# The cosine half of the rotary turn does the exchange of 64-dimension parts, and row sends move behind it

## The reference

```
def _rotate_half(x):
    d = x.shape[-1] // 2
    return jnp.concatenate([-x[..., d:], x[..., :d]], axis=-1)
...
q = q * cos + _rotate_half(q) * sin
k = k * cos + _rotate_half(k) * sin
...
scores = jnp.einsum('bqhd,bkhd->bhqk', q, k) * scale
```

## Time and profile before

| | |
|---|---|
| median of 3 runs | 1418.35 us (1413.24 to 1418.37) |
| profiled execution | 1411.39 us |
| its span, first to last instruction | 1409.6 us |
| mean granted clock of PE | 0.960 |
| PE busy | 1264.9 us, 90% |
| DVE busy | 1051.0 us, 75% |
| ACT busy | 854.4 us, 61% |
| POOL busy | 694.4 us, 49% |

### The profile page before, as it was taken

How to read it: one execution, slowest core, us unless ns; L and a number is a source line. 1 busy time by engine, 2 the same in 40 slices (tenths; PEclk the granted TensorE clock), 3 DMA queues, 4 the chain that set the end, 5 groups by cost and what they waited for, 6 DMA issues and landing times. The chain is left out here.

```text
span 1409.6 us, 28399 instructions
## 1 busy us (share of the span) xinstructions
PE 1264.9 (90%) x8780; PEld 1125.1 (80%) x8780; DVE 1051.0 (75%) x2191; ACT 854.4 (61%) x1956; POOL 694.4 (49%) x718
## 2 busy tenths in 40 slices
PE   3899999999999999999989989972997999999965
PEld 2789789889889888978978878862665999999854
DVE  3778677777787768879877878846224999999956
ACT  2666566565566556566656656634114999999832
POOL 4433433433443443344464455413713888888830
PEclk8999999999999999999999999975998999999979
DMA  7676676675467775577576577612305888888868
GB/s 241 166 184 158 172 180 157 175 200 149 120 167 191 195 197 142 140 197 181 155 198 178 131 180 194 182 59 44 107 30 156 271 271 274 269 271 268 258 203 264
DMA packets 204439, 256.48 MB, mean 182 GB/s; under 512 B 11130, under 2 KB 177694, under 8 KB 204340
## 3 DMA queue, kind: packets, MB, share of 16 engines
q1 hardware_dynamic: 193300, 229.92, 60.3%
q0 software_dynamic: 11040, 25.30, 5.5%
HBM read 90.42 MB, written 169.72 MB: 185 GB/s over the span
## 5 line engine op out<-in xcount | busy, mean ns | idle before, releaser
L764 DVE TENSOR_REDUCE neg_max<-scores 128x1 f32<-128x256 f32 (+7 forms) x256 | 193.0, 754 | 150.4 <-PE scores L880 148.5
L536 ACT ACTIVATE pt_hi<-pt 128x512 fp32r<-128x512 f32 (+3 forms) x384 | 174.7, 490 | 190.7 <-PE pt L889 189.0
L509 ACT ACTIVATE probs<-scores,neg_max 128x256 f32<-128x256 f32 (+7 forms) x256 | 190.2, 743 | 55.8 <-DVE neg_max L764 55.4
L469 POOL TENSOR_TENSOR turned<-turned,turn_sin 128x512 f32<-128x512 f32 x80 | 102.9, 1286 | 230.3 <-DVE turn_sin L708 230.3
L789 PE MATMUL o_ps<-pt_hi,v_hi 128*128 128x256 f32 (+1 forms) x640 | 193.6, 303 | 21.5 <-DVE o_lo L728 21.2
L720 DVE TENSOR_TENSOR pt_lo<-pt,pt_hi 128x512 fp32r<-128x512 f32 (+3 forms) x384 | 200.7, 551 | 13.5 <-ACT pt_hi L536 10.3
L790 PE MATMUL o_ps<-pt_lo,v_hi 128*128 128x256 f32 (+1 forms) x640 | 179.6, 281 | 0.0
L791 PE MATMUL o_ps<-pt_hi,v_lo 128*128 128x256 f32 (+1 forms) x640 | 179.3, 280 | 0.0
L466 POOL TENSOR_TENSOR turned<-taken,cos 128x512 f32<-128x512 f32 x80 | 104.1, 1301 | 144.9 <-ACT taken L519 144.7
L889 PE MATMUL pt<-ident,probs 128*128 128x128 f32 x1152 | 169.5, 274 | 5.7 <-DVE pt_lo L720 4.4
L1422 POOL DMA_INDIRECT results_dram<-y_sb,dest x134 | 148.6, 1109 | 33.7 <-issue 27.3
(11 more groups left out here) (250 smaller groups left out, 3668.9 us busy)
## 6 DMA issues: line engine op xcount, KB each, us to landing
rows_dram<-empty SPq DMA_DIRECT2D x64, 2096.2 KB
up_raw<-in_up SPq DMA_DIRECT2D x69, 368.0 KB
x_in<-rows_dram SPq DMA_DIRECT2D x68, 258.0 KB
parts<-results_dram SPq DMA_DIRECT2D x16, 768.0 KB, 9.8
down_raw<-in_down SPq DMA_DIRECT2D x69, 128.0 KB
down_raw<-in_down_tail SPq DMA_DIRECT2D x69, 112.0 KB
w_raw<-in_w SPq DMA_DIRECT2D x8, 768.0 KB, 16.5
wo_raw<-in_wo SPq DMA_DIRECT2D x8, 512.0 KB, 19.4
```

The source lines that it names most:

```text
L509: nc.scalar.activation(probs[:, at_probs(k, m), 0:w], scores_ps[m % 2][:, score_cols(m)], ACT.Exp, bias=neg_max[:, m % 4:m % 4 + 1], accum ...
L536: nc.scalar.activation(pt_hi[m // 2 % 2][:, a:z, P * (m % 2):P * (m % 2) + P], pt_ps[c % 2][:, 0:P * (z - a)].rearrange("p (k q) -> p k q" ...
L764: nc.vector.tensor_reduce(neg_max[:, n % 4:n % 4 + 1], scores_ps[n % 2][:, score_cols(n)], AX.X, ALU.max, negate=True).then_inc(max_made, 1)
```

## The change

POOL's cosine is now two instructions over 64 partitions each. They read one half of the partitions and write the other, with a wait between them, and DVE's sine is one instruction over 128 partitions without an exchange. DVE does a key's sine at the same place of the step as a query's, ahead of the reciprocal and of the addition to `resid`. Ahead of each first cosine instruction POOL waits until everything that it issued before is complete: its additions, its lower parts, and the landing of every row send. The sends are placed anew. In the first half they stood at every second step (49, 51, ..., 95); now there are two in neighbouring steps out of each four (50, 51, 54, 55, ..., 95). The other 24 stand in round 3 from its step 42 on, in three of four steps up to step 55 and in each step after it.

```
-EARLY_FILL = {step: f for f, step in enumerate([2 * STEPS + 49 + 2 * f for f in range(SENDS // 2)]
-                                               + [3 * STEPS + 41 + 2 * f for f in range(GT)]
-                                               + [3 * STEPS + 48 + f for f in range(SENDS // 2 - GT)])}
+EARLY_FILL = {step: f for f, step in enumerate([2 * STEPS + 50 + 4 * (f // 2) + f % 2 for f in range(SENDS // 2)]
+                                               + [3 * STEPS + n for n in range(41, 69) if n > 55 or n % 4 != 1])}
...
                         pool.wait_ge(proj_taken, now(k, len(ROPES), r + 1))
-                        pool.wait_ge(turn_split, now(k, len(ROPES), r - 1))
-                        nc.gpsimd.tensor_tensor(turned[r % 2][:], taken[r % 2][:], cos[:, pos], ALU.mult).then_inc(cos_made, 1)
-                        pool.wait_ge(cos_made, now(k, len(ROPES), r + 1))
+                        pool.wait_ge(turn_made, made["turn"])
+                        pool.wait_ge(turn_split, made["split"])
+                        for b in range(RING_ROWS):
+                            if made[b] > 0:
+                                pool.wait_ge(rows_sent[b], 16 * made[b])
+                        if not first:
+                            pool.wait_ge(x_split, made["x"])
+                            pool.wait_ge(w_split, made["w"])
+                            pool.wait_ge(wo_split, made["wo"])
+                        nc.gpsimd.tensor_tensor(turned[r % 2][0:64], taken[r % 2][64:128], cos[64:128, pos], ALU.mult).then_inc(cos_made, 1)
+                        pool.wait_ge(cos_made, 2 * now(k, len(ROPES), r) + 1)
+                        nc.gpsimd.tensor_tensor(turned[r % 2][64:128], taken[r % 2][0:64], cos[0:64, pos], ALU.mult).then_inc(cos_made, 1)
+                        pool.wait_ge(cos_made, 2 * now(k, len(ROPES), r + 1))
+                        made["turn"] += 1
                         pool.wait_ge(sin_made, now(k, len(ROPES), r + 1))
...
-                nc.vector.tensor_tensor(turn_sin[r % 2][0:64], taken[r % 2][64:128], sin[64:128, pos], ALU.mult)
-                nc.vector.tensor_tensor(turn_sin[r % 2][64:128], taken[r % 2][0:64], sin[0:64, pos],
-                                        ALU.mult).then_inc(sin_made, 1)
+                nc.vector.tensor_tensor(turn_sin[r % 2][:], taken[r % 2][:], sin[:, pos], ALU.mult).then_inc(sin_made, 1)
...
                     turn = fill_at(n - 2)
-                    if turn and turn[0] == "Q" and runs(turn[1], per("Q"), first, last):
+                    if turn and turn[0] in "KQ" and runs(turn[1], per(turn[0]), first, last):
                         turn_by_sine(k, *turn)
...
-                    if turn and turn[0] == "K" and runs(turn[1], per("K"), first, last):
-                        turn_by_sine(k, *turn)
```

More of the change, by code:

```diff
@@ L409, in _ @@
             pool.sem_inc(wo_split, SPLITS)
-            for s in (cos_made, turn_made, turn_split):
-                pool.sem_inc(s, len(ROPES))
+            pool.sem_inc(cos_made, 2 * len(ROPES))
+            pool.sem_inc(turn_made, len(ROPES))
+            pool.sem_inc(turn_split, len(ROPES))
+            made = {"turn": len(ROPES), "split": len(ROPES), "x": 2 * SPLITS, **{b: 0 for b in range(RING_ROWS)}}
+            for name, positions in (("w", SPLIT_W), ("wo", SPLIT_WO)):
+                made[name] = SPLITS + sum(runs(at(positions, n), SPLITS, True, False) for n in range(FIRST, FIRST + STEPS))
             pool.memset(ident[:], 0.0).then_inc(const_step, 1)
@@ L448, in send @@
                     oob_is_err=False).then_inc(rows_sent[f % RING_ROWS], 16)
+                made[f % RING_ROWS] += 1
             def body(k, first, last):
@@ L458, in body @@
                         nc.gpsimd.tensor_tensor(lo, turned[r % 2][:], hi.bitcast(F32), ALU.subtract).then_inc(turn_split, 1)
+                        made["split"] += 1
                     use = fill_at(n - 1)
@@ L472, in body @@
                         lower_parts(pool, nc.gpsimd, k, n, first, last)
+                        made["x"] += x_part(k, n, first, last) is not None
+                        for name, positions in (("w", SPLIT_W), ("wo", SPLIT_WO)):
+                            made[name] += runs(at(positions, n), SPLITS, first, last)
                     if k * STEPS + n - 1 in EARLY_FILL:
```

## The result

The changed kernel took 1438.9 us (median of 4 runs, 1438.04 to 1440.39), the kernel before 1417.39 us in the same comparison: a ratio of 1.0159, 95% interval 1.0136 to 1.0181. The forecast was 1434 us. The profiled execution took 1438.04 us, its span is 1436.2 us.

What follows compares the result with a forecast made beforehand. Attention was taken to be paced by PE, with gains only where PE waits for another engine. DVE's relief -10, start +2 and landing waits +24 gave +16 us, 1434 us on the runs' median; 8-in-10 range 1408 to 1450.

Steps and rivals of the forecast that it cites:

- Price of the halves: POOL's cosine: each 64-partition instruction was taken to cost 1.28 us, the same as a plain one over 128.
- The slow crossing: Rival on POOL's cosine: crossing partitions costs 2.6 us per half, 30 us more, 1464 us in all; chance 0.08.
- Start: First three turns, where nothing else runs: the longer cosine is on the path, +1.8 us, taken as +2.
- DVE's relief, -10: Shorter sine in attention: 5.6 us at key chunks, 3.6 at value chunks, 1 elsewhere; bounds nothing and 20 us.
- the prediction's own sign of error: Before the first send: some 5 us ahead expected; a lead over 10 us would show the prediction wrong.
- The landing waits, +24: Cosines waiting for sends make `q_lo` late for PE: 5.7, 9, 5.1 us at steps 55, 71, 87; 4.5 in round 3.
- The end, 0: End of attention: the last row copy stands one step later; nothing was counted for it.
- Landings hidden: Rival on the sends: those of the last four steps land in 2.4 to 4 us, 1413 us in all; chance 0.20.
- DVE's relief wins: Rival in attention: PE's waits for DVE fall by 20 us, landings near minimum lose 3, 1403 us; chance 0.12.

Runs made afterwards that it cites:

- same: The kernel before, unchanged, run and profiled once more: 1415.98 us.
- sine1cos2: sine1 with the whole 128-partition cosine issued twice on GpSimd; only attention compared: 12.7 us ahead of the kernel before at turn 58.
- sine1: Kernel before with DVE's sine as one 128-partition instruction, no exchange; only attention compared: 25.8 us ahead at turn 58 (1374.61 us in all, routing changed).
- keyfree: Changed kernel with three pairs of sends one step later, so no key's cosine stands right behind a send: 1425.55 us, ratio 1.005 to the kernel before.
- oldfill: Changed kernel with the row sends at their old steps, one every two steps: 1433.59 us, ratio 1.0123 to the kernel before.
- newfill: Kernel before with only its row sends moved to the changed kernel's steps: 1424.33 us, ratio 1.0065.
- keyback: Changed kernel with the key's single sine instruction back at its old place, behind `resid`: ratio 1.0174 to the kernel before.
- sine1key: sine1 with the key's sine at the changed kernel's early place; only attention compared: 22.4 us ahead of the kernel before at turn 58.
- split2: Changed kernel with the old turn form in the last round, keyfree's sends and the key's sine at its old place: ratio 0.9967 to the kernel before.
- split3: split2 with the row sends at the steps of the kernel before: 1459.37 us against 1467.5 for the kernel before, ratio 0.995.
- keypos: Kernel before with only the key's two sine instructions moved ahead of the reciprocal and `resid`: 1435.31 us, ratio 1.0135.

## Why the prediction was right, and where it was not

The direction and the place of the loss were right: it stands at steps 55, 71, 87 and 110. At the first three the cosine waits for a landing (9.20, 4.46 and 7.28 us in front of the key's, where 6 to 8 had been expected), ACT behind it at `k_hi` (7.57, 8.05 and 5.94 us), and PE behind ACT; the fourth is another matter. Against `same`, the changed kernel's profile is 22.1 us longer (1438.04 less 1415.98), and 21.5 on the medians; 16 were forecast. Point by point:

- **Price of the halves.** 1.28 us predicted, 1.27 us alone measured. The slow crossing is ruled out.
- **Start.** +2 predicted, +1.9 at turn 2, but that agreement is luck: 1.2 us of it are there at turn 0 already, before any cosine, and `same` shows 1.2 us at turn 2 too. What the change adds up to there is 0.7 us. The second cosine alone costs 2.5 us in these turns (sine1cos2 +1.8, sine1 -0.7); the shorter sine, which I had not counted here, gives 1.9 back (sine1 against `same`).
- **DVE's relief, -10.** This is the term that was mis-sized. From turn 2 to turn 58 it measured -17.7 us, and the prediction's own sign of error, a lead over 10 us before the first send, came up. I had bounded the relief by PE's waits, and PE's idle time did fall by no more than 8.1 us. The other 7.2 us came from PE's clock: before, four of PE's waits between 60 and 640 us were followed by matmuls at half speed, as behind the earlier trace rows (granted clock 0.87 and then 0.50 in the windows of 274 to 276 and 276 to 278 us; after, 1.00 throughout at that place). After, none is. Three of the four waits are gone, with 0.71 us in their stead; the fourth (2.08 us, at 503.59) is still there, and the clock stayed up behind it by chance: behind the same wait it fell in keyfree and oldfill, which issue the same instructions there. Since the kernel before has falls by chance too, its own lead is uncertain by some 5 us: against newfill's profile the changed kernel's lead is 10.9 us, against `same` 16.9. It is over 10 us by each. And I took the key's place as part of the gain: keyback and sine1key give it nothing clear. What is gained is the second sine instruction, 25.8 us, less 13.1 for GpSimd's second cosine. That cost of GpSimd in ordinary turns I had at nothing but for the first three.
- **The landing waits, +24.** Measured +30.4. By place, with my figures beside: step 55 8.7 (5.7), step 71 15.3 (9), step 87 7.2 (5.1), step 110 3.8 (4.5), the rest smaller moves both ways. The landings were not the main error: the key cosines started 10.2, 5.5 and 8.3 us behind their sends, where I had taken 8.5, 6.7 and 8.5. The error is again that I put the loss equal to PE's lateness. PE's idle time grew by 14.4 us; another 17.0 us are slower matmuls, which fits the lower clock behind the stops. keyfree shows the cause: without these sends the losses at steps 55 and 87 shrink by 6.6 and 6.7 us. The way was also another than I wrote: at steps 55, 71 and 87 PE stops at `proj_ps` for `taken` (4.51, 4.63 and 2.88 us), and at no send for `q_lo`. At step 110 the cosine is not what stops PE. Three sends in a row have left ACT without a free ring buffer; its row copy waits for a landing, `o_hi` stands behind the copy, and `o_lo` behind `o_hi`:

```profile
875.80 0.42 ACT L617 ACTIVATE early_rows<-resid 128x256 f32<-128x256 f32 x1 [2.86 <-DMA rows_dram<-early_rows,early_slots_int]
...
877.19 0.36 PE L805 MATMUL o_ps<-pt_hi,v_hi 128*128 128x256 f32 x1 [2.64 <-DVE o_lo L746]
```

PE runs again 1.2 us before the cosine does (878.38). newfill, where no cosine waits, has the same wait of ACT (1.92 us) and loses 1.9 us at this turn.
- **The end, 0.** Measured +2.5 us: the idle time ahead of the routing is longer, and it goes with the later last send: 4.97 us in split2, 2.76 in split3, which differ in the sends alone. Another 2.9 us are lost between turn 79 and the last addition to `resid` (17.4 less 14.5 us), for which the sum had nothing either.
- **Rivals.** "Landings hidden" is refuted by 78.5 us of waits. "DVE's relief wins" was nearer than I thought: the relief came near its 20 us, but what it won was lost again nearly twice over.

So the errors partly cancelled: 8 us too little gain against 6 us too little loss and 5 us at the end. That the total came within 6 us is in part luck.

## What to carry to other kernels

When a stop of PE is priced, price the matmuls behind it too: here a stop of 4.5 us cost 8.7. Behind shorter waits, of about 2 us, the clock fell in some executions and not in others, for 1.6 us each time; so a lead read from one profile is no closer than some such steps, and the same instructions are worth a second profile. Where an operation is moved to an engine that also issues scattered DMAs, ask first whether it will have to wait for their landings, and keep the old form for the stretch in which they are out. An earlier place in an engine's list is only a gain if nothing that PE needs sooner stands behind it: the same move was about neutral with one instruction (3.4 us lost and 3.0 won) and cost 18 us with two.

## What the runs showed of the hardware

- PE's granted clock fell to half (1.2 GHz) behind waits as short as 1.80 us (0.87, then 0.50) and 2.57 us (0.75, 0.50, 0.50, 0.54). Behind waits of 0.71 and 1.03 us in the changed kernel at the same place it stayed at 1.00, and behind the 1.46 us of the earlier trace rows too. It does not fall behind each wait of that size: in the kernel before it stayed at 1.00 behind 1.81 us (494.01), 2.02 (613.66) and 1.99 (842.46), in keypos once behind 2.58 us (498.22). With the same instructions it fell behind the wait at 165 us before and not in newfill. Behind the six waits of 4.51 to 9.75 us that PE had beside the sends in the changed kernel, keyfree and oldfill it was at 0.50 each time. I had not expected that waits of 2 us count.
- A GpSimd multiplication over 64 partitions that reads the other half's partitions costs as much as a plain one over 128 (1.27 against 1.28 us).
- A second GpSimd instruction of 1.3 us in each turn cost 13 us over 58 turns, though GpSimd is busy only 55% of the stretch from 60 to 640 us (317.00 of 580 us). Its hold on DVE is a path that shows: 50 sines took 46.8 instead of 34.5 us. In the first ten turns, 5.6 of the 13 us, the longer cosine itself may be on the path; that was not taken apart.
